# Three stages do their own normalisation inside their first products, the attention steps are re-cut to equal TensorE work, and the gated products are unrolled

## The reference, cut to what matters

```python
x = x + sublayer(_layernorm(x), ...)            # twelve times

def _layernorm(x, eps=1e-05):
    m = mean(x); v = var(x)                     # over the 128 features
    return (x - m) / sqrt(v + eps)
```

```python
q = xn @ Wq; k, v = split(context @ Wkv)        # one key/value head
out = softmax(q k^T / 8) v @ Wo
gate, value = split(xn @ Wff1); out += (silu(gate) * value) @ Wff2
```

```python
scores = q k^T / 8 + bias * 2.0 ** -(head + 1)
out = softmax(scores) v @ W_out + b_out
```

## Time and profile before

| what | value |
|---|---|
| median of 3 runs | 1850.88 us (1845.6 to 1854.02) |
| the profiled execution's own time | 1855.54 us |
| its span, first to last instruction | 1853.7 us |
| TensorE busy | 1561.6 us (84%) |
| VectorE busy | 1199.7 us (65%) |
| ScalarE busy | 885.2 us (48%) |
| GpSimd busy | 663.4 us (36%) |
| mean granted TensorE clock | 0.927 of full speed |

### The profile page before, as it was taken

One profiled execution on the slowest core, in us unless ns is written; L12 is line 12 of the kernel. 1 busy time (PEld: TensorE's weight loads), 2 busy tenths in 40 slices (PEclk: granted clock), 3 DMA queues, 4 the chain that ended last, 5 costly groups with the idle time before them and its releaser, 6 DMA issues. The chain is left out here.

```text
span 1853.7 us, 29578 instructions
## 1 busy us (share of the span) xinstructions
PE 1561.6 (84%) x10155; PEld 997.7 (54%) x10155; DVE 1199.7 (65%) x2484; ACT 885.2 (48%) x2473; POOL 663.4 (36%) x619
## 2 busy tenths in 40 slices
PE   5998858699799997979999889999855589489998
PEld 2565535455577765533333367777633234367776
DVE  4897562488678865438988966666676467723333
ACT  3664432277565552237677645566521244233332
POOL 2557340224554423138888942222501300300000
PEclk9999977799999999979999989999987799579999
DMA  6000000000000000020000000000000000000000
GB/s 267 2 2 2 1 1 1 0 1 2 1 1 2 2 1 1 1 81 1 0 1 1 1 1 1 1 1 2 1 1 0 1 1 1 0 1 1 0 0 23
DMA packets 2725, 18.84 MB, mean 10 GB/s; under 512 B 544, under 2 KB 672, under 8 KB 1696
## 3 DMA queue, kind: packets, MB, share of 16 engines
q1 hardware_dynamic: 2592, 17.14, 2.3%
HBM read 16.09 MB, written 1.05 MB: 9 GB/s over the span
## 5 line engine op out<-in xcount | busy, mean ns | idle before, releaser
L727 POOL TENSOR_TENSOR l_xattn_probs<-l_xattn_probs,l_xattn_recip 128x512 f32<-128x512 f32 x128 | 140.9, 1101 | 271.0 <-DVE l_xattn_recip L711 271.0
L895 ACT ACTIVATE l_attn_probs<-ps,l_attn_neg_max 128x128 f32<-128x128 f32 x512 | 144.7, 383 | 81.9 <-DVE l_attn_neg_max L944 81.4
L2409 POOL TENSOR_TENSOR l_mamba_hc<-l_mamba_h,l_mamba_c 128x512 f32<-128x512 f32 x128 | 158.9, 1267 | 0.0
L2311 DVE TENSOR_TENSOR_SCAN l_mamba_h<-ps,l_mamba_dBx 128x512 f32<-128x512 f32 x128 | 152.7, 1212 | 1.8 <-ACT ps L2208 0.7
L2081 PE MATMUL ps<-l_mamba_hc,w_const 128*128 128x512 f32 x256 | 136.6, 637 | 19.5 <-POOL l_mamba_hc L2409 16.5
L3080 DVE SCALAR_TENSOR_TENSOR xn<-ps,l_moe_gates,xn 128x128 f32 x224 | 63.1, 344 | 138.4 <-PE ps L3004 138.4
L3050 ACT ACTIVATE l_moe_hidden<-ps,w_early 128x512 f32<-128x512 f32 x112 | 70.7, 683 | 117.1 <-PE ps L2986 117.1
L3004 PEld LDWEIGHTS ps<-w_early,l_moe_hidden 128*128 128x128 f32 x896 | 109.6, 194 | 29.5 <-issue 21.6
L3004 PE MATMUL ps<-w_early,l_moe_hidden 128*128 128x128 f32 x896 | 110.2, 277 | 4.6 <-ACT l_moe_hidden L3050 4.6
L2986 PE MATMUL ps<-xnT,w_early 128*128 (+1 forms) x224 | 108.1, 609 | 0.0
L245 POOL TENSOR_TENSOR rs<-rs,neg_half 128x12 f32<-128x12 f32 (+2 forms) x22 | 36.7, 1669 | 195.6 <-DVE rs L239 195.6
(11 more groups left out here) (493 smaller groups left out, 3675.8 us busy)
## 6 DMA issues: line engine op xcount, KB each, us to landing
w_early<-in_l_moe SPq DMA_DIRECT2D x1, 3669.0 KB, 11.2
w_l_xattn<-in_l_xattn SPq DMA_DIRECT2D x1, 2176.0 KB, 22.5
w_early<-in_l_xattn SPq DMA_DIRECT2D x1, 1890.0 KB, 15.3
w_l_attn<-in_l_attn SPq DMA_DIRECT2D x1, 1242.0 KB, 24.3
ctx<-in_ctx SPq DMA_DIRECT2D x1, 1088.0 KB, 11.1
x<-in_x SPq DMA_DIRECT2D x2, 512.0 KB, 4.5
ctxT<-in_ctxT SPq DMA_DIRECT2D x1, 1024.0 KB, 9.0
out_x<-x SPq DMA_DIRECT2D x1, 1024.0 KB, 3.9
```

What stands on the lines that cost most here:

```text
L727: nc.gpsimd.tensor_tensor(probs[:, t % 4, :, :], probs[:, t % 4, :, :], along(recip[:, t % 2, :], [P, 4, P]), ALU.mult)\
L895: ins = nc.scalar.activation(probs[:, t % 4, g, :], S_of(t)[:, g * P:(g + 1) * P], ACT.Exp, bias=neg_max[:, t % 2, g:g + 1], accum_out=total)
L2311: nc.vector.tensor_tensor_scan(flat(h[:, t % 2, half, :, :]), G.ps[:, DA_BANK[half], :], flat(dBx[:, t % 2, half, :, :]), 0.0, ALU.mult, A ...
L2409: nc.gpsimd.tensor_tensor(heads4(hc[:, t % 4, half, :]), h[:, t % 2, half, :, :], c_sb[:, t % 3, :, :], ALU.mult).then_inc((hc0_set, hc1_s ...
```

## The change

`Lead` takes the place of the `layernorm` block in `l1_xattn`, `l1_ffn` and `l2_xattn`. Each quad is transposed by TensorE when the stage needs it, between its own products: quads 0 and 1 at the start, quads 2 and 3 during the first steps. What is left of the normalisation is the first thing on VectorE and GpSimd, and the last four tiles come behind the stage's first products. The 16 scalings of layer 2's bias are spread over the first four steps.

In the diff `begun(t)` is `finished(t + 1)`. `finish` is halved over the steps with u = 0 and u = 1, and the projections move: in layer 1 from steps 1, 2, 3 to 2, 2, 3, in layer 2 from steps 0, 0, 1, 2, 2, 3 to 1, 2, 2, 3, 3 and the first step of the tile itself, in a new order. At u = 1 the projection comes last, behind `finish`.

`swiglu` loses its loops, has two buffers for `hidden` and two output banks, and issues `down` of a quad behind the second pair of the next one. `l1_ffn` splits the last part of `prepare` off as `place_rows`, behind the big products of `up`.

```diff
+class Lead:
+    def __init__(self, nc, G, s, weights, banks, gT=None, bT=None):
...
+        self.rest = Rest(nc, G, s, begun)
+    def tensor(self, pe, q):
+        self.rest.wait_normed(pe, q)
+        if self.banks[q] in self.banks[:q]:
+            pe.wait_ge(self.stored, q)
+        for j in range(QUAD):
+            mm = nc.tensor.transpose(G.ps[:, self.banks[q], j * P:(j + 1) * P], G.xn[:, q * QUAD + j, :], G.c["ident"])
+        mm.then_inc(self.turned, 1)
+    def scalar(self, act, q):
+        act.wait_ge(self.turned, q + 1)
+        dst, bank = G.xnT[:, q * QUAD:(q + 1) * QUAD, :], heads4(G.ps[:, self.banks[q], :])
+        if self.gT is None:
+            nc.scalar.copy(dst, bank).then_inc(self.stored, 1)
+        else:
+            nc.scalar.activation(dst, bank, ACT.Identity, bias=self.bT, scale=self.gT).then_inc(self.stored, 1)
+    def wait(self, eng, b):
+        eng.wait_ge(self.stored, b // QUAD + 1)
...
 def wide_attention
+        lead = Lead(nc, G, s, cfg.tag, (2, 3, 5, 5), gT, bT)
...
-            return [(n, name, b + 1) for n, (name, step, _) in enumerate(cfg.proj) if step == u and b + 1 < NB]
+            due = [(n, name, b + 1 - step // U) for n, (name, step, _) in enumerate(cfg.proj) if step % U == u]
+            return [(n, name, b_) for n, name, b_ in due if 0 < b_ < NB]
...
-            order += [("out", finished(t))] if finished(t) is not None else []
+            order += [("out", begun(t))] if begun(t) is not None else []    
...
-            def finish(b):
-                pe.wait_ge(o_copied, 2 * (b + 1))
-                wait_taken(pe, place["out", b] - 2)
-                for c in range(8):
+            def finish(b, half):
+                pe.wait_ge(o_copied, 2 * b + half + 1)
+                if half == 0:
+                    wait_taken(pe, place["out", b] - 2)
+                for c in range(4 * half, 4 * half + 4):
...
             for n in range(n_proj):
+                if names[n] == "q0":
+                    lead.tensor(pe, 0)
                 project(n, 0)
+            lead.tensor(pe, 1)
             for t in range(STEPS + V_LAG + 2):
                 if t < STEPS:
                     scores(t)
-                    for n, name, b in at_step(t):
-                        project(n, b)
+                    if t == 1:
+                        lead.tensor(pe, 2)
+                    if t == 3:
+                        lead.tensor(pe, 3)
+                    if finished(t) is None:
+                        for n, name, b in at_step(t):
+                            project(n, b)
...
+                if begun(t) is not None:
+                    finish(begun(t), 0)
                 if finished(t) is not None:
-                    finish(finished(t))
+                    finish(finished(t), 1)
+                    if t < STEPS:
+                        for n, name, b in at_step(t):
+                            project(n, b)
...
 def l1_xattn
-            tag="l1_xattn", kvT=G.wkv, own_keys=False, proj=[("q0", 1, "A"), ("q1", 2, "A"), ("kv", 3, "V")],
+            tag="l1_xattn", kvT=G.wkv, own_keys=False, proj=[("q0", 2, "A"), ("kv", 2, "V"), ("q1", 3, "A")],
 def l2_xattn
-            proj=[("q0", 0, "A"), ("k0", 0, "V"), ("q1", 1, "A"), ("k1", 2, "V"), ("v0", 2, "A"), ("v1", 3, "A")],
+            proj=[("k0", 1, "V"), ("q0", 2, "A"), ("q1", 2, "A"), ("k1", 3, "V"), ("v0", 3, "A"), ("v1", 4, "A")],
...
 def swiglu, TensorE
-            up(0, (0, 1))
-            with pe.Fori(0, NQ - 1) as q:
-                up(q, (2, 3))
-                up(q + 1, (0, 1))
-                down(q)
-            up(NQ - 1, (2, 3))
-            down(NQ - 1)
+            for n in range(NQ * CH + 2):
+                if n < NQ * CH:
+                    up(n)
+                if n >= CH and n % CH == 1:
+                    down(n // CH - 1)
 def swiglu, VectorE, per pair n
+                if n > CH and c == 1:
+                    add(q - 1)
...
+            ahead.variances(dve)
+            ahead.apply(dve, nc.vector, 6)
+            add(LAST)
...
 def l1_ffn, TensorE
+            lead.tensor(pe, 0)
+            lead.tensor(pe, 1)
             prepare(0)
             up(0)
             prepare(1)
+            lead.tensor(pe, 2)
             for q in range(NQ):
                 if q + 1 < NQ:
                     up(q + 1)
+                if q == 0:
+                    lead.tensor(pe, 3)
                 down(q)
```

More of the change, by code:

```diff
@@ L670, in _ @@
         def _(dve):
+            lead.rest.early(dve, nc.vector, 0, 0)
+            lead.rest.variances(dve)
+            for q in range(1, NQ):
+                lead.rest.early(dve, nc.vector, 0, q)
             for n, name in enumerate(names):
                 take(dve, "V", n, name, 0)
+            if cfg.bias_ready:
+                lead.needs(dve)
             for t in range(STEPS + V_LAG + 3):
+                if t < U and cfg.bias_ready:
+                    cfg.bias_ready(dve, t)
                 if t < STEPS:
@@ L713, in _ @@
                     ahead.variances(dve)
+                if t == 1:
+                    lead.rest.late(dve, nc.vector, 0)
                 if cfg.beside and t < STEPS:
@@ L718, in _ @@
         def _(pool):
+            lead.rest.early(pool, nc.gpsimd, 1)
+            lead.rest.scales(pool)
+            lead.rest.late(pool, nc.gpsimd, 1)
             if cfg.b_out is not None:
@@ L1206, in _, with add @@
         @block.vector
         def _(dve):
-            def body(q):
-                for c in range(CH):
-                    dve.wait_ge(gated, CH * q + c + 1)
-                    after(dve, out_made, q)
-                    nc.vector.tensor_tensor(hidden[:, c, :], gate[:, c % 2, :], G.ps[:, 2 * (c % 2) + 1, :],
-                                            ALU.mult).then_inc(multiplied, 1)
-                    if q == 0:
-                        for half in range(2):
-                            wkv.scan(dve, LAST, c, half)
-                    if q == 1 and c < 2:
-                        wkv.sum(dve, LAST, c)
-                    if 2 <= CH * q + c - 4 < 2 + QUAD:
-                        j = CH * q + c - 6
-                        wkv.invert(dve, LAST, slice(j * P, (j + 1) * P))
-                    seen_behind(dve, ahead, added, q, c)
-                if q == NQ - 1:
-                    ahead.apply(dve, nc.vector, 8)
+            def add(q):
@@ L1271, in l1_ffn, with _ @@
         block = s.block()
+        @block.sync
+        def _(sp):
+            lead.sync(sp)
         @block.gpsimd
         def _(pool):
+            lead.needs(pool)
+            lead.rest.early(pool, nc.gpsimd, 1)
+            lead.rest.scales(pool)
+            lead.rest.late(pool, nc.gpsimd, 1)
             for q in range(NQ):
+                pool.wait_ge(lead.stored, q + 1)
                 quad = slice(q * QUAD, (q + 1) * QUAD)
@@ L1382, in seen @@
                     ahead.variances(dve)
+            lead.needs(dve)
+            lead.rest.early(dve, nc.vector, 0, 0)
+            lead.rest.early(dve, nc.vector, 0, 1)
+            lead.rest.variances(dve)
+            lead.rest.early(dve, nc.vector, 0, 2)
             take(0)
+            lead.rest.late(dve, nc.vector, 0)
             take(1)
```

142 lines of the change are left out of this document (99 added, 43 removed).

## The result

The changed kernel took 1876.6 us (median; 1870.6 to 1886.4), the kernel before 1852.4 beside it: ratio 1.0143, interval 1.009 to 1.0196. It is slower by about 24 us, where I had forecast 6. The profiled execution spans 1877.4 us, 23.7 more than that of before.

| stretch | before | after | difference | forecast |
|---|---|---|---|---|
| start to layer 1's wide attention (first transposes) | 476.1 | 469.2 | -6.9 | 0 |
| its opening, to the first scores | 12.7 | 6.5 | -6.2 | -6.4 |
| scores to its end: twelve tiles | 146.1 | 152.1 | +6.0 | -2.1 |
| the rest of it | 48.7 | 51.1 | +2.4 | +1.7 |
| `swiglu`, to `l1_ffn`'s transposes | 51.7 | 47.5 | -4.2 | -3.7 |

What follows compares the result with a forecast made beforehand. TensorE's instruction order was taken to bound the kernel, gaps counting where TensorE waits. Terms +22.7 - 2.1 - 3.7 - 6.4 + 1.7 - 4.6 - 3.8 + 3.2 - 0.8 = +6.2 on 1850.9 gave 1857 us, range 1844 to 1868.

Steps and rivals of the forecast that it cites:

- Layer 2's tile, order: Layer 2's attention: 13 gaps grow from 0.79 to 2.52 us as TensorE's query product awaits the addition to `x`; +22.7 us.
- Chain: Layer 2's tile: VectorE's key copy, transposes' copy, reciprocal, bias, maximum and addition, then TensorE; 3.17 us from key projection's issue end.
- Layer 2's tile, clock: Layer 2's repeating tile: the forecast sum held no term for a fall of TensorE's clock; 0 us.
- rival C: Layer 2's attention: TensorE's clock falls in the repeating gap, giving 1883 us; chance 0.04.
- C's own price of 26: Layer 2's attention: some 4 us of work taking twice as long after each gap, priced as 13 x 2 = 26 us.
- Layer 1's tile: Layer 1's attention: twelve repeating tiles shorten from 146.1 to 144.0 us through fewer waits; -2.1 us.
- My bounds 0 and 8: Layer 1's twelve tiles: gain of 0 if waits stay unchanged in number, 8 us if all waits go.
- `swiglu` (-3.7): `swiglu`: moving `down` behind the next quad's second pair removes three 1.47 us gaps, with about 1.5 given back; -3.7 us.
- My 3.8 for it: `swiglu`: sum would be 3.8 us lower if the skill page's budget counted in full for three table loads; forecast gave nothing.
- Openings: Openings of three stages: layer 1's attention -6.4, +1.7 given back; `l1_ffn` -4.6; layer 2's attention -3.8, +3.2 and -0.8.
- The +3.2 in my sum: Layer 2's attention opening, given back: 1.06 us of transposes and two waits of about 0.9 for ScalarE's copies; +3.2 us.
- Untouched stages: Start, mamba stage and the part behind layer 2's attention: no term in the forecast; 0 us.

Runs made afterwards that it cites:

- layer 1's table alone: Changed kernel with layer 2's attention order put back and layer 1's output product in one piece, its new projection table kept: 1848.2 us, ratio 0.998.
- the first of the two faster versions: Changed kernel with both attention orders put back and layer 2's addition to `x` ahead of the bias addition on VectorE: 1824.8 us, ratio 0.9868.
- the one with the addition to `x` first: Changed kernel with one edit: in layer 2's attention VectorE adds to `x` ahead of bias addition and maximum: 1853.2 us, ratio 1.0026.
- split-only kernel: Changed kernel with layer 2's order back and layer 1's old projection table, its output product still split in halves: 1862.3 us, ratio 1.0044.

## Why the prediction was wrong

**Layer 2's tile, order (forecast +22.7): right.** 13 x 1.67 = 21.7. Chain, place, count and releaser were as described; the chain was 0.14 us shorter.

**Layer 2's tile, clock (forecast 0): the step that failed.** I set rival C aside with "it stayed at 1.00 through `swiglu` with 1.47 us gaps, but none of 2.5 us repeats before", and gave it 0.04. The first half was true and said nothing on 2.3 us: in this place the clock holds at waits of 0.99 and 1.59 and falls at 2.31. It cost 13 x 1.49 = 19.4 us, more than the whole miss of 17.5; other misses partly cancel. C's own price of 26 doesn't follow from its sentence: 4 us of work at half the clock would cost 4 us a time, not 2. The trace agrees in kind with the warning of the Trainium skill ("TensorE: Matmul & The Clock Gate", HAM oscillation) that gaps which recur bring the half clock back each time, here 0.66 behind a wait. It differs in size: the page tells it of longer gaps than 2.31 us, so it did not settle the case either way. I had outweighed the warning by the absence of such gaps before, though the change itself made them. With no row against it at that size, C deserved a third or more, and the range should have reached 1885.

**Layer 1's tile (-2.1, measured +6.0): wrong in sign.** The wait for `l_xattn_oT` stayed (5.0 us in 14, as 5.4 before). I had priced the halved product at nothing per tile: from start to start its halves take 1.09 us each where the whole took 1.98, 2.4 us more in twelve tiles. And "the addition to `x` is now needed about 1.06 us behind the scores" held for a free VectorE only: where a 1.32 us scan stands ahead, TensorE waits 2.15 and then runs slower, 3.8 us in that tile against its neighbours. My bounds 0 and 8 both lay on the gain's side.

**`swiglu` (-3.7): right, -4.2.** The three waits are gone, and the end gives back 1.1 of it. From the end of the attention to the last output product the rows show 5.26 us less. The three waits are 4.31 of it (1.47, 1.46, 1.38); the rest is spread over products that now follow each other more closely (a down-projection's 3.73 us is 3.57 from its start to the next one's). So nothing is left over that could be the table loads (four before, one now): they were hidden, and the estimate by the Trainium skill's "ScalarE: Activation LUTs" (What ACT_TABLE_LOAD costs) would have been wrong here. My 3.8 for it was also three bare loads of 1.28; with the drain that the page adds, the estimate by it is 8.0. The trace of before shows no such drain: the load of the earlier trace rows ends at 694.29, and ScalarE's next SiLU starts at 694.30.

**Openings.** Layer 1's: -6.2 for -6.4, given back 2.4 for 1.7. `l1_ffn`: -2.7 for -4.6; the half clock still came. Layer 2's: -6.7 for -3.8, with 3.9 for 2.4 given back. I had costed part of the projections at half clock; it was 1.00 from the first of them on. The +3.2 in my sum was also too much for its own terms, 1.06 + 2 x 0.9 = 2.9. Together -9.3 by the rows, -10.7 forecast. No run takes these openings back by themselves, so that they cause it is read from rows, not tested.

**Untouched stages (0, measured -9.8)** hid part of the loss, by luck as far as the runs show: -6.9 at the start, -4.2 in the mamba stage, +1.3 at the end. The misses add up: 18.4 in layer 2's tiles, 8.1 in layer 1's, 1.4 in the openings, -0.5 in `swiglu`, -9.8 here, 17.6, against 23.7 - 6.2 = 17.5.

## What to carry to other kernels

A wait on TensorE can cost twice: its own length, and the half clock behind it. Here 0.7 us more wait cost 2.2, and useless products in the gap made the kernel faster. So ask of each new gap whether gaps of its size stand in the trace at full clock, and count "none of that size" as open, not as evidence. A gap of that size with full clock behind it is weak evidence too, as the next section shows. When an order of work is changed around a small ring of banks, look at which instruction stands two entries behind the slow consumer, and move that consumer's instruction first in its engine's queue: that one edit took 37 us off the stage in the changed kernel and 12.2 with the order of before, 1.6 of them from the clock in the opening.

## What the hardware showed that I had not expected

The step between 1.59 and 2.31 us of wait in layer 2's tile: tiles of 16.57 us with clock 1.00 on one side, of 18.7 to 19.1 with 0.91 on the other. What lies between them was not tried.

The length of one wait isn't all that decides. The opening of layer 2's attention has the same waits in several kernels (0.61, 0.37, 0.49, then 1.4 us). TensorE behind the last of them, first with layer 1's table alone, then in the first of the two faster versions:

```profile
1094.27 0.71 PE L633 MATMUL ps<-l_xattn_probsT,l_xattn_v 128*64 128x128 f32 x8 [1.41 <-ACT xnT L371]
1094.90 1.23 PE L607 MATMUL ps<-l_xattn_k,l_xattn_q 64*128 64x128 f32 x8
1096.06 2.07 PE L588 MATMUL ps<-xnT,w_l_xattn 128*128 128x128 f32 x8
```

```profile
1080.83 0.66 PE L633 MATMUL ps<-l_xattn_probsT,l_xattn_v 128*64 128x128 f32 x8 [1.40 <-ACT xnT L371]
1081.42 0.71 PE L607 MATMUL ps<-l_xattn_k,l_xattn_q 64*128 64x128 f32 x8
1082.07 1.16 PE L588 MATMUL ps<-xnT,w_l_xattn 128*128 128x128 f32 x8
```

The granted clock is 0.50 in the 3.2 us behind the first of these waits and 1.00 in the 3.4 us behind the second. The same happens to a wait of 2.15 us in the mamba stage: four products behind it take 1.93 us in the changed kernel (clock 1.00) and 2.96 us (0.63) in the one with the addition to `x` first. Why, no run here tells.

The granted clock of the mamba stage's first 30 us lies between 0.66 and 0.83 over the profiles, for the same instructions; between the kernel before and the changed one that is 3.6 us. And single executions of one kernel differ by more than the edits of some runs: the split-only kernel's ten lie at 1853 to 1869 us, with a mean granted clock of 0.932 to 0.933 in the three at 1853 and of 0.920 to 0.925 in the seven above 1858.
